# Scores and row maxima of grouped attention moved from one 96-row product to two 64-row tiles of the array

## What is computed

```python
xn = _layernorm(x); x = x + attn0(xn) + ffn0(xn)    # full softmax, scale 1/4; gelu, 2048 wide
xn = _layernorm(x); x = x + attn1(xn) + ffn1(xn)    # rotary, causal, scale 1/16; silu gate, 512 wide
scores = q @ k.T * scale        # 32 query heads of 16 elements, 8 key heads, 4 query heads to a key head
probs = softmax(scores); ctx = probs @ v; out = ctx @ Wo.T
```

## Time and profile before

| | |
|---|---|
| median of 3 runs | 596.59 us (593.41 to 599.78) |
| the profiled execution, its own time | 596.43 us |
| its span in the trace | 594.7 us |
| granted TensorE clock, mean | 0.997 of full speed |
| TensorE matmul busy | 563.2 us (95%) |
| TensorE weight load busy | 435.0 us (73%) |
| VectorE busy | 456.5 us (77%) |
| ScalarE busy | 348.0 us (59%) |
| GpSimd busy | 232.6 us (39%) |

### The profile page before, as it was taken

How to read it: one execution, slowest core, us unless ns; L and a number is a source line. 1 busy time by engine, 2 the same in 40 slices (tenths; PEclk the granted TensorE clock), 3 DMA queues, 4 the chain that set the end, 5 groups by cost and what they waited for, 6 DMA issues and landing times.

```text
span 594.7 us, 10503 instructions
## 1 busy us (share of the span) xinstructions
PE 563.2 (95%) x3216; PEld 435.0 (73%) x3216; DVE 456.5 (77%) x1232; ACT 348.0 (59%) x598; POOL 232.6 (39%) x345
## 2 busy tenths in 40 slices
PE   3979999999999999999999999899899999998997
PEld 3967777777777878777787787667677778766754
DVE  6487987765666687577899678898998989789673
ACT  3667756664564676376677276357645564565451
POOL 6231334713304521313223115264745485364242
PEclk9999999999999999999999999999999999999999
DMA  6993452453223244315433323336443443434101
GB/s 200 130 317 103 120 142 69 113 157 107 79 82 108 80 124 136 90 40 174 126 128 99 113 78 101 90 107 143 134 117 89 104 130 109 125 108 133 29 6 68
DMA packets 30535, 67.02 MB, mean 113 GB/s; under 512 B 4880, under 2 KB 18192, under 8 KB 28560
## 3 DMA queue, kind: packets, MB, share of 16 engines
q1 hardware_dynamic: 21840, 38.04, 24.5%
q0 software_dynamic: 8640, 28.32, 15.9%
HBM read 50.87 MB, written 13.63 MB: 108 GB/s over the span
## 4 chain that ended last, share of the span: by engine, by line
PE 79%; DVE 8%; issue 5%; DMA 3%; POOL 2%; ACT 2%; DVEq 0%; POOLq 0%; ACTq 0%
PE banks L766 53%; PE banks L826 8%; PE banks L874 8%; PE banks L852 7%; DMA q_sb<-max_t 2%; DVE banks L1156 2%; PE banks L786 1%; PE banks L855 1%; POOL probs L708 1%; DVE neg_max L1156 1%; DVE o_tok L1177 1%; DVE x_res L1200 1%; PE banks L835 1%; DVE bn L1054 1%; DVE hid L1221 1%
## 5 line engine op out<-in xcount | busy, mean ns | idle before, releaser
L988 ACT ACTIVATE probs<-banks 128x512 f32<-128x512 f32 (+1 forms) x256 | 138.0, 545 | 187.5 <-PE banks L852 149.2
L766 PE MATMUL banks<-xnT,w_up 128*128 128x512 f32 x576 | 153.8, 400 | 0.2
L1161 DVE TENSOR_REDUCE neg_max<-banks 128x2 f32<-128x512 f32 x128 | 87.4, 688 | 79.3 <-PE banks L826 77.9
L766 PE MATMUL banks<-w_down,hid 128*128 128x512 f32 x480 | 127.4, 399 | 0.0
L766 PEld LDWEIGHTS banks<-xnT,w_up 128*128 128x128 f32 x576 | 102.1, 190 | 30.6 <-issue 12.9
L826 PEld LDWEIGHTS banks<-k_sb,q_sb 96*128 96x128 f32 x512 | 92.5, 191 | 23.6 <-issue 5.5
L1156 DVE CUSTOM_DVE_ANT_0 banks<-banks,mask_qk 128x128 f32<-128x128 f32 (+1 forms) x256 | 86.3, 375 | 25.5 <-PE banks L826 24.9
L826 PE MATMUL banks<-k_sb,q_sb 96*128 96x256 f32 (+1 forms) x512 | 100.0, 277 | 5.4 <-issue 3.2
L766 PEld LDWEIGHTS banks<-w_down,hid 128*128 128x128 f32 x480 | 85.2, 188 | 25.7 <-DVE max_t L1169 5.9
L708 POOL TENSOR_SCALAR_AFFINE_SELECT probs<-probs 128x256 f32<-128x256 f32 x128 | 59.5, 465 | 75.9 <-ACT probs L988 69.3
L852 PE MATMUL banks<-q_sb,k_sb 97*128 97x512 f32 x192 | 78.8, 410 | 8.4 <-DMA q_sb<-max_t 7.0
(11 more groups left out here) (79 smaller groups left out, 655.3 us busy)
## 6 DMA issues: line engine op xcount, KB each, us to landing
q_sb<-q_parts SPq DMA_DIRECT2D x60, 256.0 KB, 4.8
raw<-in_up POOLq DMA_DIRECT2D x48, 256.0 KB, 3.4
raw<-in_down POOLq DMA_DIRECT2D x40, 256.0 KB, 3.1
q_parts<-stage SPq DMA_DIRECT2D x30, 256.0 KB, 2.5
raw<-in_attn POOLq DMA_DIRECT2D x20, 256.0 KB, 3.6
k_parts<-stage SPq DMA_DIRECT2D x14, 256.0 KB, 2.5
k_sb<-k_parts SPq DMA_DIRECT2D x14, 256.0 KB, 4.1
out<-x_res SPq DMA_DIRECT2D x8, 256.0 KB, 2.1
```

The costliest lines, as they stand in the source:

```text
L766: mm = nc.tensor.matmul(out_ap, lhs(a), rhs(b_), start=first and j == 0, stop=stop and j == 2, **kw)
L988: nc.scalar.activation(probs[:, i, 0:w], banks[:, ST_BANKS[k % 2], 0:w], ACT.Exp, scale=SCALES[n // B]).then_inc(exp_done, 1)
L1161: nc.vector.tensor_reduce(neg_max[:, s, 2 * g:2 * g + 2, t], banks[:, bank_of[x], :].rearrange("p (r t) -> p r t", r=2)[:, :, 0:w], AX.X, ...
```

## The change

The parts are stacked in 48 rows: queries hi, lo, hi and keys hi, hi, lo, so the product lo·lo is left out. The maximum's row is row 48. The four key heads of a unit are laid out in two halves of the partitions: rows 0 to 48 hold the first of each pair, rows 64 to 112 the second. The query and key tiles are half as wide. Each `m` and `st` step handles two key heads (four query heads) with two tiles of 64 rows and two banks. So a unit has four `m` and four `st` steps, and they stand in the even slots. `st` waits until both exponentials of the step before are done. The two `mrow` rows are two DMAs; `load_q` is four DMAs and 384 KB of rows where it was two and 512 KB; `load_k` is two and 192 KB where it was one and 256 KB; the first k and q take 6 and 12 DMAs. The zero rows and their fills go; GpSimd sets rows 32 to 63 and 96 to 127 of the key tile to one, before the loads. The planned costs of an `st` and an `m` step become 340. The value matmuls, the fill-in work and its slots stay.

```diff
-ROWS = 96
-MROW = 96
+HALF = 64
+ROWS = 48
+MROW = 48
+STEPS = 4
...
-    slots = [[("st", u, i)] for i in range(8)]
+    slots = [[] for i in range(8)]
     for i in range(8):
-        if i < 4 and u + 1 < UNITS:
-            slots[i].append(("m", u + 1, i + 4))
-        if i >= 4 and u + 2 < UNITS:
-            slots[i].append(("m", u + 2, i - 4))
+        j = i // 2
+        if i % 2 == 0:
+            slots[i].append(("st", u, j))
+        if i in (0, 2) and u + 1 < UNITS:
+            slots[i].append(("m", u + 1, j + 2))
+        if i in (4, 6) and u + 2 < UNITS:
+            slots[i].append(("m", u + 2, j - 2))
...
                     if x == ("store", 0, 2):
...
+                        sp_.wait_ge(made, K_ONES)
+                        for a in range(2):
+                            for e, h in enumerate(K_PARTS):
+                                at = HALF * a + HD * e
+                                sp_.dma_start(k_sb[at:at + HD, :, :].bitcast(F32), half[a][:, h, 0, :]).then_inc(first_k, 16)
...
+                    for a in range(2):
+                        src = qscr0[n, s, a] if n < B else qscr1[n - B, s, :, a, :]
+                        to = q_sb[HALF * a:HALF * a + ROWS, u % RING, :, :].rearrange("p c t -> p (c t)").bitcast(F32)
+                        sp_.dma_start(to[0:2 * HD], src).then_inc(q_loaded[u % RING], 16)
+                        sp_.dma_start(to[2 * HD:], src[0:HD]).then_inc(q_loaded[u % RING], 16)
...
+                    for a in range(2):
+                        row = HALF * a + MROW
+                        sp_.dma_start(q_sb[row:row + 1, u % RING, :, :].rearrange("o c t -> o (c t)").bitcast(F32),
+                                      max_t[8 * a:8 * a + 8, u % 2, :].bitcast(F32)).then_inc(m_loaded[u % RING], 16)
...
                     for r in range(2):
-                        mm = nc.tensor.matmul(banks[:, k, r * T:r * T + w],
-                                              q_sb[0:ROWS, u % RING, 2 * g + r, t * P:t * P + P], k_sb[0:ROWS, 4 * f + g, 0:w],
-                                              start=r == 0, stop=r == 1, skip_group_check=True)
+                        for a in range(2):
+                            rows = slice(HALF * a, HALF * a + ROWS)
+                            mm = nc.tensor.matmul(banks[:, ks[a], r * T:r * T + w],
+                                                  q_sb[rows, u % RING, 2 * c + r, t * P:t * P + P], k_sb[rows, 2 * f + c, 0:w],
+                                                  start=r == 0, stop=r == 1, skip_group_check=True)
                     mm.then_inc(wk_filled, 1)
...
+                    if st_index(u, j):
+                        pe.wait_ge(exp_done, 2 * st_index(u, j))
...
+                    for a in range(2):
+                        rows = slice(HALF * a, HALF * a + MROW + 1)
+                        mm = nc.tensor.matmul(banks[:, ST_BANKS[a], 0:2 * (T - q0)].rearrange("p (r t) -> p r t", r=2),
+                                              k_sb[rows, 2 * f + c, t * P:t * P + P],
+                                              q_sb[rows, u % RING, 2 * c:2 * c + 2, q0:], start=True, stop=True)
                     mm.then_inc(st_filled, 1)
...
-                    nc.scalar.activation(probs[:, i, 0:w], banks[:, ST_BANKS[k % 2], 0:w], ACT.Exp,
-                                         scale=SCALES[n // B]).then_inc(exp_done, 1)
+                    for a in range(2):
+                        nc.scalar.activation(probs[:, 2 * j + a, 0:w], banks[:, ST_BANKS[a], 0:w], ACT.Exp,
+                                             scale=SCALES[n // B]).then_inc(exp_done, 1)
```

More of the change, by code:

```diff
@@ L39 @@
 RING = 3
+Q_PARTS = (0, 1, 0)
+K_PARTS = (0, 0, 1)
 ST_BANKS = (0, 1)
@@ L142, in start_slots @@
     o += [parts(("qkv", 0, 1)) + [("v", 0)]]
[L143 to L152, removed]
+    o += [parts(("up", 0, 0, 0)) + [("load_q", 2)], parts(("up", 0, 1, 0))]
+    ms = spread([[("m", 0, j)] if j < 4 else [] for j in range(5)], parts(("qkv", 1, 2)), [1] * 5)
+    ms += spread([[("m", 1, 0)], [], [("m", 1, 1)], []], parts(("qkv", 1, 0)), [1] * 4)
+    ms[4].append(("mrow", 0))
+    ms[5] += [("mt", 0), ("load_bias",)]
+    ms[6] += split(0, "up", 2, 3)
+    ms[7] += split(0, "down", 0, 1)
     return o + ms
@@ L300, in work_banks @@
         if (x in wk or x[0] == "up") and x not in bank:
-            k = [k for k in recent if k not in taken][0]
+            uses = [x + (a,) for a in range(2)] if x[0] == "m" else [x]
+            before[x] = []
+            for y in uses:
+                k = [k for k in recent if k not in taken][0]
+                recent.remove(k)
+                recent.append(k)
+                if k in user:
+                    before[x].append(user[k])
+                bank[y], user[k] = k, y
+                taken.add(k)
+            bank[x] = [bank[y] for y in uses] if x[0] == "m" else bank[x]
+        for y in emptied_by(step):
+            k = bank[y]
+            taken.remove(k)
             recent.remove(k)
             recent.append(k)
[L304 to L311, removed]
     return bank, before
@@ L320, in emptied_by @@
 def emptied_by(step):
-    if step[0] in ("m", "mt", "v", "wo") or step[0] == "qkv" and not direct(step):
-        return step
+    if step[0] == "m":
+        return [step + (a,) for a in range(2)]
+    if step[0] in ("mt", "v", "wo") or step[0] == "qkv" and not direct(step):
+        return [step]
     if step[0] == "drain" and (step[1][0] == "xn" or direct(step[1])):
-        return step[1]
+        return [step[1]]
     if step[0] == "add":
-        return ("down",) + step[1:]
+        return [("down",) + step[1:]]
     if step[0] == "gate":
-        return "up", 1, step[1], 0
+        return [("up", 1, step[1], 0)]
     if step[0] == "hidden":
-        return ("up",) + step[1:] + (step[1],)
-    return None
+        return [("up",) + step[1:] + (step[1],)]
+    return []
 def low_on_dve(x):
@@ L346, in build @@
     wk = numbered(order, "m", "mt", "xn", "qkv", "v", "wo", "down")
-    em = {x: k for k, x in enumerate(y for y in map(emptied_by, order) if y and y[0] != "up" and (y[0] != "qkv" or direct(y)))}
+    em = {x: k for k, x in enumerate(y for z in order for y in emptied_by(z) if y[0] != "up" and (y[0] != "qkv" or direct(y)))}
     cp = numbered(order, "xn", "qkv")
@@ L758, in work @@
             def work(x):
-                if before[x]:
-                    wait_fill_read(pe, before[x])
+                for y in before[x]:
+                    wait_fill_read(pe, y)
                 return bank_of[x]
@@ L926, in _ @@
                     nc.scalar.copy(to[0], raw[:, k % RAW, :]).then_inc(hi_split, 1)
-                if x[0] == "fill":
-                    act.wait_ge(made, 1)
-                    nc.scalar.copy(q_sb[64:ROWS, x[1], :, :].rearrange("p g t -> p (g t)"),
-                                   zero[64:ROWS, :].to_broadcast([ROWS - 64, UH * T])).then_inc(q_zeroed, 1)
                 if x[0] == "root":
```

205 lines of the change are left out of this document (100 added, 105 removed).

## The result

The changed kernel takes 604.5 us (median of 4 runs, 602.23 to 609.12), the kernel before 595.0 beside it. The ratio is 1.0156, 95% interval 1.0097 to 1.0214: slower by 1.6%, where I had forecast 2.7% faster. The profiled execution took 609.12 us with a span of 607.3 us; it is the slowest of the four, and its mean granted clock the lowest, 0.974. The others had 0.983, 0.986 and 0.986 with spans of 604.3, 601.1 and 600.4 us. So part of what is to be explained may lie in TensorE's clock.

A forecast was written before the change was run, and what follows sets the result against it. The prediction took TensorE, busy 95% of the span, as the bound, with VectorE close in layer 1. Layer 0 -13.4, layer 1 -4 and the start +1.4 made -16.0 us, from 596.4 to 580 us, range 564 to 600.

The forecast's parts named there:

- Overlap of the tiles: In `st` and `m` steps: two 64-row tiles stream side by side, `st` 0.235 us for 0.47, `m` 0.27 us.
- The bound for the weight loads: In an `m` step of four matmuls: weight loads going one after another at 0.085 us give 0.34 us.
- One way in and one way out serve both: 0.235 us: On TensorE, around neighbouring `st` and `m`: changing the array's division costs 0.235 us, four times a unit; ends 0 and 0.47.
- Layer 1: TensorE's steps there: 3.08 us a unit becomes 2.57, 8 us in 16 units, of which half, 4 us, was counted.
- Loads and stores: I count 0: SyncE's queue: two more `load_q` issues of 0.4 to 0.6 us stay covered; without cover 1 us a unit.
- The second DMA for the maxima: the two cancel nearly: Before `st`: issued some 0.5 us later, against `mt` 0.3 to 0.4 us earlier; counted 0, ends 0 and 8 us.
- Work banks, count 0: An `m` step takes two of five banks at once; the next `m` is over 3 us later, so no cost.
- ScalarE and the `st` banks: `st` waits for both exponentials of the step before; it just fits, misses under 1 us a unit, counted 0.
- The start: First k and q loads take more issues, so the first `m` begins later: +1.4 us, ends 0 and 3.
- layer 1 turns around VectorE: Rival, chance 0.10: maxima arrive late in every layer 1 unit, 0.5 to 1 us each, giving 588 to 597 us.
- The slower side: Rival, chance 0.10: tiles that divide the array's rows do not run side by side, 628 us, or 600 with partial overlap.
- the rival in which everything overlaps: Rival, chance 0.19: `m` at 0.24 us and the division half hidden, about 567 us; sign: a pair at 0.68 or less.

## Why the prediction was wrong, point by point

- **Overlap of the tiles.** Right, and complete: 0.57 against 0.34 in the run with both in one half. The bound for the weight loads (0.34 for four) did not bind in the wide steps, by the lone `st` and `m` of 0.43 each.
- **"One way in and one way out serve both: 0.235 us".** This is the step that failed in layer 0: the term was mis-sized and measures 0.4. The way in, read from `pv` behind an `m` step (0.08), was right; it is 0.1 here. The way out was not: I took only what `pv` holds within its own 1.00 us and not the 0.1 us that the full matmuls behind it take more, which the trace of before had (three of them 0.80 us behind `pv`, 0.70 behind `m`). The 0.07 us that remain, 0.4 less 0.33, are within the group; why, no run shows. With 0.88 in place of 0.74 for the pair the gain of layer 0 is 64 x 0.07 = 4.5 us in place of 13.4. Without waits and half clock the traces show 5.8.
- **Layer 1.** By the steps' own distances the 0.5 us a unit were not there: with 0.4 a group, 3.14 against 3.08 us. The rest without waits and half clock did shrink by 7.8 us, for which part of the reason is open. What failed is the half that I counted as kept: waits grew by 7.7 us and half clock took up to 10.2, and the layer lost 10.
- **"Loads and stores: I count 0".** Failed. I had counted the issues of the q load, and noted that the order of the queue is the same. I did not add the k store and k load that stand ahead of it in one unit of four, 10 issues for 5. Five waits of up to 2.0 us, 6.5 in all, came of it, one of them with 6.8 us at half clock; moving the load one slot was worth 5.5 us by the medians.
- **"The second DMA for the maxima: the two cancel nearly".** Not settled: removing it took 2.3 us off the wait and 0.4% off the time, within the noise of the two ratios. That lies between my two ends, 0 and 8 us.
- **Work banks, count 0.** Failed with the burst as a whole. The grouping of `m` alone costs 2.6%, both groupings 1.2%, with the same number of bank uses; the wait of 2.7 us in the changed kernel, with 3.4 us at half clock behind it, stands in the trace with both groupings and no tiles as well. Whether the two banks at once do it or VectorE's four operations in a row, the runs don't separate; the stretched entries speak for the banks.
- **ScalarE and the `st` banks.** Right: 2.7 us of waiting in all, and `st` in pairs was harmless or slightly good.
- **The start.** I had +1.4 us; the first `st` came 0.7 us earlier (41.04 for 41.73). The DMAs were half as large and landed in 2.6 us in the median, for 6.3.
- **The clock.** It has no term in my sum. Five of seven waits of about 2 us brought 3.4 to 10.2 us at half clock. 31 us at half clock cost up to 15 us in the profiled execution, against under 2 before, and the runs of the changed kernel stand in the order of their clocks.
- **The rivals.** That layer 1 turns around VectorE was the nearest, for the maxima that arrive late. I stopped at 597 because I added its loss to a gain that was only partly there. The slower side as I had put it was refuted; the slower result came by small waits that I had each priced at nothing.

What I had named as signs of an error were the right ones in part: the pair of steps did cost more than 0.85, if the 0.2 us around it are counted. By the distance that I had named, 0.68, the sign pointed the wrong way, at the rival in which everything overlaps.

## What to carry to other kernels

Price a division of the array by the starts on both sides of the group: here the full matmuls ahead of it carry a quarter of the cost, and those behind it another. Put all steps that divide the array next to each other, rows and columns alike, and only where the engines that read the results have room; a pair of steps that saves 0.475 us of streaming keeps 0.07 when it pays 0.4 for its group. When one transfer becomes two or four, add up the issues of everything ahead of it in the queue, in the unit where most coincide. And on a kernel that keeps TensorE busy all the time, give a new wait of 2 us a price for the clock as well: over the seven of this trace, half clock cost up to 15 us for 15 us of waiting, so about twice the length in all.

## What the runs showed of the hardware that was not expected

- Two tiles of 64 rows with 512 columns each take the time of one (0.34 us to the next tiled step; 0.57 if both use the same half).
- Going from full matmuls to tiles and back costs 0.4 us: 0.1 in the full matmuls ahead, 0.2 in the group and 0.1 in the full matmuls behind; from row tiles straight to column tiles no extra shows (0.34 to the start of `pv`).
- A wait of 2.03 us of TensorE was followed by 6.8 us at 1.2 GHz, one of 2.25 us (to 392.2 us) by 10.2 us, and one of 2.02 us (to 287.7 us) by none.
- A DMA of 8 KB whose two destination rows are 64 partitions apart works as one issue: 0.52 us of SyncE's queue where two DMAs took 1.3.
